# Two router gates in a four-layer kernel: which operand of the gate matmul stands still

## What is computed

```python
# mixture 0, on x normalised (4096 tokens of 256)
scores = softmax(x @ gate_w + gate_b)         # gate_w 256 x 8, gate_b 8
weights, indices = top_k(scores, 2)
# mixture 1, on x normalised
gate_logits = einsum('bnd,de->bne', x, gate_w)   # gate_w 256 x 8, no bias
competitive_gates = sinkhorn(gate_logits)
```

## Time and profile before

| | us |
|---|---|
| median of 3 runs | 2303.82 |
| lowest, highest | 2302.01, 2306.51 |
| the profiled execution | 2325.94 |
| its span, first to last instruction | 2324.2 |
| granted clock of PE, mean share | 0.915 |

### The profile page before, as it was taken

How to read it: one execution, slowest core, us unless ns; L and a number is a source line. 1 busy time by engine, 2 the same in 40 slices (tenths; PEclk the granted TensorE clock), 3 DMA queues, 4 the chain that set the end, 5 groups by cost and what they waited for, 6 DMA issues and landing times. The chain is left out here.

```text
span 2324.2 us, 48998 instructions
## 1 busy us (share of the span) xinstructions
PE 1967.9 (85%) x18133; PEld 1328.0 (57%) x18133; DVE 1704.7 (73%) x2695; ACT 1216.9 (52%) x2198; POOL 475.0 (20%) x608
## 2 busy tenths in 40 slices
PE   5888888799899999989888899999999999861270
PEld 4666666478799999968777333343343343330150
DVE  6667676667578888846644799999999999657822
ACT  4555555333266666622233288888888888620010
POOL 1010100100122233124343112212212212300054
PEclk9999999799899999989999599999999999875585
DMA  2000000461143333333278897774763701020054
GB/s 92 2 0 0 0 0 0 180 246 57 67 159 110 115 118 113 105 106 112 71 238 267 96 83 64 62 45 43 62 47 41 62 20 38 19 73 0 8 178 140
DMA packets 222808, 188.18 MB, mean 81 GB/s; under 512 B 121532, under 2 KB 201368, under 8 KB 220504
## 3 DMA queue, kind: packets, MB, share of 16 engines
q1 hardware_dynamic: 202872, 146.71, 31.7%
q0 software_dynamic: 18080, 27.17, 4.5%
q10 hardware_dynamic: 1728, 12.58, 1.6%
HBM read 121.37 MB, written 64.75 MB: 80 GB/s over the span
## 5 line engine op out<-in xcount | busy, mean ns | idle before, releaser
L2032 ACT ACTIVATE ga_probT<-banks 128x512 f32<-128x512 f32 x1024 | 557.0, 598 | 154.3 <-PE banks L2092 104.2
L1989 DVE TENSOR_REDUCE ga_nmax<-banks 128x1 fp32r<-128x1024 f32 x512 | 610.5, 1219 | 19.6 <-PE banks L2079 18.3
L2079 PE MATMUL banks<-a_ks,a_qs 48*128 48x512 f32 x1024 | 386.5, 460 | 9.7 <-PEq L77 5.6
L2092 PE MATMUL banks<-a_qs,a_ks 49*128 49x512 f32 x1024 | 379.8, 451 | 2.3 <-ACT ga_probT L2032 2.3
L2109 PE MATMUL banks<-ga_probT,a_v 128*32 128x256 f32 x4096 | 331.1, 396 | 6.4 <-ACT ga_o L2038 6.4
L2079 PEld LDWEIGHTS banks<-a_ks,a_qs 48*128 48x128 f32 x1024 | 156.9, 192 | 221.4 <-DVE ga_nmax L1989 175.5
L1955 POOL DMA_DIRECT2D a_qs<-ga_max_rows x256 | 131.4, 521 | 569.7 <-DVE ga_max_rows L1996 528.6
L1450 PE MATMUL banks<-rb_xT,rb_own_w 128*128 128x256 f32 x1872 | 232.2, 283 | 4.6 <-DVE rb_xT L1316 3.7
L1450 PEld LDWEIGHTS banks<-rb_xT,rb_own_w 128*128 128x128 f32 x1872 | 224.7, 190 | 10.7 <-issue 6.7
L2109 PEld LDWEIGHTS banks<-ga_probT,a_v 128*32 128x32 f32 x4096 | 81.4, 108 | 196.9 <-ACT ga_probT L2032 153.1
L1156 PE MATMUL banks<-m_xnT,sh_w 128*128 128x512 f32 x768 | 184.8, 399 | 6.5 <-DVE sh_w L945 5.3
(11 more groups left out here) (326 smaller groups left out, 3203.5 us busy)
## 6 DMA issues: line engine op xcount, KB each, us to landing
rb_w_f<-in_L_ffn_rw_dram SPq DMA_DIRECT2D x39, 512.0 KB
m_xnT<-xnT_parts ACTq DMA_DIRECT2D x12, 1024.0 KB, 4.9
sorted_out<-rb_yb SPq DMA_DIRECT2D x39, 256.0 KB, 2.1
m_w<-in_L_ffn_rw_dram SPq DMA_DIRECT2D x2, 4096.0 KB, 19.9
values<-pg_v SPq DMA_DIRECT2D x16, 512.0 KB, 3.1
a_v<-values SPq DMA_DIRECT2D x16, 512.0 KB, 8.9
a_qs<-queries_rounded SPq DMA_DIRECT2D x28, 256.0 KB, 8.8
a_ks<-keys_rounded SPq DMA_DIRECT2D x28, 256.0 KB, 9.8
```

The source lines that it names most:

```text
L1989: nc.vector.tensor_reduce(nmax[b % 2][:, at:at + 1], slot[:], axis=AX.X, op=ALU.max, negate=True).then_inc(use_read, 1)
L2032: nc.scalar.activation(probT[k % SETS][2 * h + n][:], b_t[ring_place["weights", w] % RING][:], ACT.Exp, scale=SCALE).then_inc(exp_ready, 1)
L2079: return nc.tensor.matmul(slot[:, HALF * kh:HALF * (kh + 1)], qs[a][rows, n, P * q:P * (q + 1)], ks[a][rows, n, HALF * kh:HALF * (kh + 1)] ...
L2092: nc.tensor.matmul(bank[:], ks[a][rows, 2 * gp + n, P * kt:P * (kt + 1)], qs[a][rows, 2 * gp + n, HALF * hf:HALF * (hf + 1)], start=True, ...
```

## The change

In both phases the operands of the gate matmul change places. The transposed tile (128 hidden columns x 128 tokens) is the stationary operand and the gate's 8 columns move, so the product has the 128 tokens on partitions. A step issues 8 matmuls with 8 moving columns instead of 2 with 512. The products of all 32 tiles go to one PSUM bank, 8 columns each, 256 in all, and stay there until the phase ends. `lT`, the turns, the copies per step and their semaphores go. In mixture 0 one DVE addition over 128x256 adds the bias, which is loaded once to each of 128 partitions, behind all of DVE's other work; in mixture 1 one ACT copy over 128x256 takes the logits out. `gw` in mixture 0 is 8 columns wide, and POOL's two memsets and SP's wait for them go.

```diff
@@ normalised_tiles
-        gw = sb("gw", [P, KD, P])
-        gb = sb("gb", [P, 1])
+        gw = sb("gw", [P, KD, E])
+        gb = sb("gb", [P, E])
...
-            sp.wait_ge(gate_zero, ONE + 2)
-            sp.dma_start(gw[:, :, 0:E], gate.rearrange("(k p) e -> p k e", p=P)).then_inc(gate_in, 16)
-            sp.dma_start(gb[0:E], gate_b.rearrange("(e o) -> e o", o=1)).then_inc(gate_in, 16)
+            sp.dma_start(gw[:], gate.rearrange("(k p) e -> p k e", p=P)).then_inc(gate_in, 16)
+            sp.dma_start(gb[:], gate_b.rearrange("(o e) -> o e", o=1).broadcast_to([P, E])).then_inc(gate_in, 16)
...
+            dve.wait_ge(gate_done, ONE + STEPS)
+            nc.vector.tensor_tensor(logits[:], b_l[:, 0:T * E].rearrange("p (t e) -> p t e", t=T),
+                                    gb[:].unsqueeze(1).broadcast_to([P, T, E]), ALU.add).then_inc(l_ready, 1)
...
-            for i in range(STEPS + 2):
-                if i < STEPS:
-                    transposed(i)
-                if 1 <= i <= STEPS:
-                    biased(i - 1)
-                if i >= 2:
-                    kept(i - 2)
+            for i in range(STEPS):
+                transposed(i)
...
-            nc.gpsimd.memset(gw[:], 0.0).then_inc(gate_zero, 1)
-            nc.gpsimd.memset(gb[:], 0.0).then_inc(gate_zero, 1)
...
                 pe.wait_ge(xnT_ready, ONE + HALVES * (i + 1))
-                if i >= 2:
-                    pe.wait_ge(lT_ready, ONE + i - 1)
-                for k in range(KD):
-                    last = nc.tensor.matmul(b_g[i % 2], gw[:, k, :], xnT[i % 2][:, k, :], start=(k == 0), stop=(k == KD - 1))
+                for c in range(C):
+                    at = E * (C * i + c)
+                    for k in range(KD):
+                        last = nc.tensor.matmul(b_l[:, at:at + E], xnT[i % 2][:, k, P * c:P * (c + 1)], gw[:, k, :],
+                                                start=(k == 0), stop=(k == KD - 1))
                 last.then_inc(gate_done, 1)
...
-            for i in range(STEPS + 2):
+            for i in range(STEPS + 1):
                 if i < STEPS:
                     transposes(i)
-                if 1 <= i <= STEPS:
+                if i >= 1:
                     gates(i - 1)
-                if i >= 2:
-                    turned(i - 2)
@@ gated_tiles: gates and PE's loop as above; on ACT
-            for i in range(STEPS + 2):
-                if i < STEPS:
-                    transposed(i)
+            for i in range(STEPS):
+                transposed(i)
                 if i == 0:
                     closing.on_scalar(act, 1, READY)
-                if 1 <= i <= STEPS:
-                    gated(i - 1)
-                if i >= 2:
-                    kept(i - 2)
+            act.wait_ge(gate_done, ONE + STEPS)
+            nc.scalar.activation(logits[:], b_l[:, 0:T * E].rearrange("p (t e) -> p t e", t=T), ACT.Copy).then_inc(l_ready, 1)
```

More of the change, by code:

```diff
@@ L679, in normalised_tiles @@
         xn = [sb(f"xn{u}", [P, C, D]) for u in range(2)]
-        gw = sb("gw", [P, KD, P])
-        gb = sb("gb", [P, 1])
+        gw = sb("gw", [P, KD, E])
+        gb = sb("gb", [P, E])
         xnT = [sb(f"xnT{u}", [P, KD, C * P]) for u in range(2)]
-        lT = [sb(f"lT{u}", [P, C * P]) for u in range(2)]
         closing = Closing(nc, g, sb, sem)
-        gate_zero, gate_in, shared_in = sem("gate_zero"), sem("gate_in"), sem("shared_in")
+        gate_in, shared_in = sem("gate_in"), sem("shared_in")
         parts_kept, rows_kept = shared.parts_kept, shared.rows_kept
@@ L689, in normalised_tiles @@
             sem(n) for n in ("xn_ready", "xnT_done", "xnT_ready", "hi_ready", "lo_ready")]
-        gate_done, lT_ready, l_done, l_ready = [sem(n) for n in ("gate_done", "lT_ready", "l_done", "l_ready")]
+        gate_done, l_ready = sem("gate_done"), sem("l_ready")
         block = begin()
         b_tp = [g.bank[2 * u:2 * u + 2] for u in range(2)]
-        b_g, b_l = g.bank[4:6], g.bank[6:8]
+        b_l = g.bank[4]
         half = lambda h: slice(TH * P * h, TH * P * (h + 1))
@@ L747, in transposed @@
                                          ACT.Identity).then_inc(xnT_ready, 1)
-            def biased(i):
-                act.wait_ge(gate_done, ONE + i + 1)
-                act.wait_ge(gate_in, ONE + 32)
-                if i >= 2:
[L753 to L759, removed]
-            closing.on_scalar(act)
-            for i in range(STEPS + 2):
-                if i < STEPS:
-                    transposed(i)
-                if 1 <= i <= STEPS:
-                    biased(i - 1)
-                if i >= 2:
-                    kept(i - 2)
+            closing.on_scalar(act)
+            for i in range(STEPS):
+                transposed(i)
         @block.gpsimd
         def _(pool):
-            nc.gpsimd.memset(gw[:], 0.0).then_inc(gate_zero, 1)
-            nc.gpsimd.memset(gb[:], 0.0).then_inc(gate_zero, 1)
             for i in range(STEPS):
@@ L2178, in gated_tiles @@
         xnT = [sb(f"xnT{u}", [P, KD, C * P]) for u in range(2)]
-        lT = [sb(f"lT{u}", [E, C * P]) for u in range(2)]
         closing = Closing(nc, g, sb, sem)
@@ L2286, in gates @@
                 pe.wait_ge(xnT_ready, ONE + HALVES * (i + 1))
[L2287 to L2290, removed]
-                last.then_inc(gate_done, 1)
[L2293 to L2301, removed]
+                for c in range(C):
+                    at = E * (C * i + c)
+                    for k in range(KD):
+                        last = nc.tensor.matmul(b_l[:, at:at + E], xnT[i % 2][:, k, P * c:P * (c + 1)], gw[:, k, :],
+                                                start=(k == 0), stop=(k == KD - 1))
+                last.then_inc(gate_done, 1)
+            for i in range(STEPS + 1):
                 if i < STEPS:
                     transposes(i)
-                if 1 <= i <= STEPS:
+                if i >= 1:
                     gates(i - 1)
-                if i >= 2:
-                    turned(i - 2)
 def attention1(nc, g, project, gate, logits, rows):
```

7 lines of the change are left out of this document (removed).

## The result

| | before | after |
|---|---|---|
| median, us | 2304.22 | 2324.14 |
| lowest, highest | 2299.42, 2317.05 | 2320.79, 2332.41 |
| runs | 6 | 6 |
| ratio, 95% interval | | 1.0085 [1.0055, 1.0116] |
| span of the profiled execution | 2324.2 | 2319.3 |

The changed kernel is slower: the medians lie 19.9 us apart, and the ratio says 0.85%, 19.6 us of 2304.22. The forecast of 2299.7 had the wrong sign; the result lies 1.7 us under the 2325.8 of rival 1.

What follows compares the result with a forecast made beforehand. PE was taken to bound the kernel, with transfers limiting mixture 0's middle. Gains of 1.4 us in mixture 0 and 2.7 in mixture 1 sum to 4.1: 2303.82 to 2299.7 us; own range 2298 to 2302, 8-in-10 range 2297.5 to 2328.

Steps and rivals of the forecast that it cites:

- rival 1: Both gate stages: PE's clock falls to 1.2 GHz, steps of 5.35 us, +22 us, 2325.8; chance 0.32.
- the condition under the sum: Both gate stages: the 4.1 us gain holds only if PE keeps 2.4 GHz; forecast's chance 0.55.
- The price of a gate matmul: New gates on PE: 0.12 us a load (0.107 to 0.135), 1.92 us a group of 16, replacing 2.16.
- Mixture 0: First gate stage: gain of 1.4 us, 0.2 from its head and 1.2 from its end.
- The end: Mixture 0 from the gates of step 6 to the phase's end: 5.7 us becomes 4.5, gain 1.2.
- the head: Mixture 0's start: SP's 0.4 us wait for POOL's memsets goes; 0.2 us reaches the phase's end.
- the middle: Mixture 0's steps: 2.82 instead of 3.03 us on PE, but transfers hold DVE, so gain 0.
- The bias' load: Mixture 0's head: 128 short pieces instead of 8; landing 0.4 us slower takes nothing from DVE's rows.
- Mixture 1: Second gate stage, bound by PE: gains of 0.4 in step 2, 1.3 over four periods, 1.0 at the end; 2.7 us.
- Rival 2: Only one gate stage loses the clock, or both for a part: +9 us, 2313; chance 0.07.
- Rival 3: New gates' loads come at 0.06 us, a group 1.0 us, gain about 10 us, 2293.8; chance 0.05.
- rival 4: Loads and streams stand in a row, 6.2 us a group instead of 2.16, about 2364 us; chance 0.01.

Runs made afterwards that it cites:

- 128 columns: Changed kernel with each gate matmul moving the gate's 8 columns 16 times over, same loads, in both phases: 2306.33 us, ratio 0.9985.
- the late bias: Kernel with 128 columns, PE waiting for mixture 0's gate and bias only ahead of its first gates: 2298.1 us, ratio 0.9983.
- 32 columns: Changed kernel with each gate matmul moving the gate's 8 columns 4 times over, same loads: 2321.49 us, ratio 1.0076.
- four streams: Changed kernel plus four fp32 matmuls of 128 moving columns a step, one per tile, products unread: 2376.86 us, ratio 1.0188.
- 96 columns again: Second visit of the changed kernel with the gate's 8 columns moved 12 times over: 2318.09 us, ratio 0.9964.

## Why the prediction failed, point by point

**The step that failed** is the condition under the sum, that PE keeps 2.4 GHz. The forecast gave it 0.55 against 0.32 for rival 1. The row that pointed the right way was there: top_tokens at 0.50 with many loads and hardly any moving columns. I set it aside with two arguments. The first was that the array idles between those short loads while the new gates would load back to back. The runs contradict it: after the change PEld has records for 18.00 of 18 us, and the clock is 0.50. The second was that mixture 1's clock rose while its gates filled only 8 of the array's 128 columns, so the amount of arithmetic isn't what counts. Whether that is so was not tried; but what those gates do have is 512 moving columns each, and it is the moving that the change takes away. If anything the argument spoke for the rival, and I counted it against it. The Trainium skill (TensorE: Matmul & The Clock Gate, Part 1) says that the throttled state is the default and that activity releases it; with records for loading in all 18.00 us and the clock at 0.50, loading doesn't do for it here.

**The price of a gate matmul.** Taken 0.12 us a load, measured 0.111 at full clock (the group at 2064.49) and in all the kernels with more columns. It lies inside the bounds of 0.107 and 0.135 and close to the lower, so a group is 1.78 us, not 1.92. At half clock 0.225 was taken and 0.214 measured. Two figures of the forecast don't add up as they stand, and neither matters: a step of mixture 0 is 0.87 + 1.92 = 2.79 us, not 2.82, and the eight groups that give 5.8 us at 0.107 give 2.2 us at 0.135, not 1.9.

**Mixture 0.** At full clock the stage gains 2.0 us (36.8 to 34.8, with 128 columns) where 1.4 were forecast. The end gives 1.5 (5.7 us before from the gates of step 6 to the last logits, 4.2 with 128 columns, 463.19 to 467.38) where 1.2 were forecast; the cheaper loads are that difference. The other 0.5 is what the last transposes start earlier in the stage, where 0.2 were forecast; how much of it the head gives wasn't measured. In the middle PE waits for DVE and DVE for the row writes, as forecast. The bias' load in 128 pieces was granted 0.4 us, what SP's wait had cost; it took more. PE's first transposes start 3.3 us into the phase (434.06 to 437.32) where they started after 2.6 (437.79, the memset at 435.22). The kernel with the late bias shows that it costs nothing while the transfers limit.

**Mixture 1.** When the clock comes back it gains 3.5 to 4.6 us (38.7 to between 35.2 and 34.1) where 2.7 were forecast. The step is 2.66 or 2.63 us instead of 2.87, five times 0.2, and that is the cheaper load. The rest moves with the time at which the clock comes back, which differed from execution to execution.

**Rival 1, by its own steps.** Forecast: a step of 5.35 us, +11.5 and +11.2, -0.7. Measured: steps of 5.01, +9.3 and +9.3. Of a step 1.74 are transposes (454.30 to 456.04) and 3.27 the gates (456.04 to 459.31); I had taken 1.75 and 3.6, so the error is in the gates, 0.34 a step and 1.7 over five steps. The load price makes 16 x 0.011 = 0.18 of it; the rest is that the next transposes' loads start before a full 0.214 us has passed since the group's last. That and 0.3 in the last two groups is what the rival was too dear by, nearly; so its total of 2325.8 lies close to the result partly since the time between the stages, which it left alone, came out 1.7 us longer. That it decides for the whole stage, since nothing in the stage raises the clock again, held in mixture 0, in mixture 1 and in the kernel with 32 columns.

**Rival 2**, one stage only, didn't occur: both stages lost the clock, and with the change in one stage alone each costs its half. **Rival 3**, loads at 0.06 us, and **rival 4**, 0.39, are both excluded by 0.111. The Trainium skill (same page, Part 3) lets a load overlap a running matmul only in another row group. In the kernel with 128 columns the 16 pairs of a group take 1.79 us (2083.99 to 2085.78), 0.112 us a pair, all on all 128 rows, while one record of load lasts 0.19 us and a stream of 128 columns is, by the 0.43 us that before's streams of 512 take each, about 0.107 us by estimate: loads and streams overlap, and the measurement decides against that rule.

**The small steps.** SP's wait on the memsets is gone, the addition on DVE took 0.42 us and the copy on ACT 0.38, as priced.

## What to carry to other kernels

Making the narrow operand the moving one buys short streams with full loads. Before doing it, look at what else moves in that stretch: if PE's clock there was at 2.4 GHz because of the streams that go away, the load price doubles, and here that cost 9.3 us a stage where the edit itself was worth 2 to 4.5. Where the loads set the pace, columns that are moved in their shadow cost nothing: moving the 8 columns 12 times over turned a loss of 0.85% into a gain of 0.3%. Extra streams set between or behind the loads, which cost time of their own, made it worse still (a loss of 1.4 and 1.9%).

## What the runs showed of the chip that was not expected

- Records for PE and PEld at 100% of a stretch say nothing about the clock: 18.00 and 18.00 of 18 us at 0.50 after the change, 15.00 and 12.94 at 1.00 with 128 columns.
- Where the clock comes back after a fall depends on the execution. In full attention's first stretch every kernel has the same program, PE is busy throughout in the windows below, and yet the clock was back at 1330 us in before and only past 1360 in the kernel with the change in mixture 1 alone. Windows of before, then of that kernel:

```profile
1330.00:1340.00 10.00, 10.00 (x100) 3.64 (x96) 9.55 (x9) 8.25 (x16) 3.38 (x7) 0.98 0.53 41
1350.00:1360.00 10.00, 10.00 (x102) 3.73 (x104) 9.83 (x11) 8.86 (x17) 4.10 (x8) 1.00 0.55 27
```

```profile
1330.00:1340.00 10.00, 10.00 (x60) 3.30 (x52) 5.90 (x6) 4.62 (x10) 4.08 (x8) 0.50 0.55 29
1350.00:1360.00 10.00, 10.00 (x56) 3.40 (x60) 5.32 (x6) 4.96 (x10) 0.00 (x0) 0.50 0.83 44
```

The stretch between the two gate stages took 1573 to 1590 us, and its length goes with the clock: 1589.8 us with 128 columns, 1577.8 with 128 columns and the late bias, two kernels with the same program there, of which the first had the clock at 0.50 for 169 us of it and the second for 140. That is why effects of 2 us were read from stage lengths rather than from times.

- The last phase took 93 to 96 us in nine profiled executions and 119 to 120 in three, of the kernel before and of changed ones alike, at a lower rate of transfers. It seems to go with the chip or the occasion rather than with the kernel: the two experiments with 119 to 120 us (four streams, and 96 columns again) are those beside which the kernel before took 2330.16 us, where it took 2304 to 2308 beside all others, and the profiled execution of before lies 20 us above its runs without a profiler. The cause was not tried.
